# Writing out the loop over pairs of token tiles in the last stage of a two-layer kernel

## What is computed

```python
x = x + L0_attn(layernorm(x), ...)   # state mixing with N = 16
x = x + L0_ffn(layernorm(x), ...)    # 9 experts, top 2
x = x + L1_attn(layernorm(x), ...)   # 16 heads, causal
x = x + L1_ffn(layernorm(x), ...)    # 64 experts, top 8, and a shared one
```

```python
shared = silu(xf @ Ws_up) @ Ws_down
aff = xf @ centroids.T
_, idx = top_k(aff + expert_biases, 8)
w = sigmoid(take_along_axis(aff, idx, axis=1));  w = w / (sum(w) + 1e-08)
cw = zeros((T, E)).at[arange(T)[:, None], idx].add(w)
h = silu(einsum('td,edf->etf', xf, W_up))
routed = einsum('etd,te->td', einsum('etf,efd->etd', h, W_down), cw)
return shared + routed
```

## Time and profile before

| What | Value |
|---|---|
| median of 3 runs (lowest, highest) | 1024.24 us (1022.57, 1024.37) |
| the profiled execution | 1021.6 us |
| its span | 1019.9 us |
| mean granted TensorE clock | 0.956 |
| PE busy | 946.4 us, 93% of the span |
| DVE busy | 825.4 us, 81% |
| ACT busy | 700.0 us, 69% |
| POOL busy | 480.2 us, 47% |

### The profile page before, as it was taken

How to read it: one execution, slowest core, us unless ns; L and a number is a source line. 1 busy time by engine, 2 the same in 40 slices (tenths; PEclk the granted TensorE clock), 3 DMA queues, 4 the chain that set the end, 5 groups by cost and what they waited for, 6 DMA issues and landing times.

```text
span 1019.9 us, 20123 instructions
## 1 busy us (share of the span) xinstructions
PE 946.4 (93%) x6082; PEld 754.9 (74%) x6115; DVE 825.4 (81%) x1938; ACT 700.0 (69%) x1394; POOL 480.2 (47%) x550
## 2 busy tenths in 40 slices
PE   3686999999789999999999979999999999999997
PEld 2564998999657677767776657787877777778786
DVE  6888776777778888888887668989898889898865
ACT  3763554555467777877787657777777778777875
POOL 3278782107456565656553404444444444444443
PEclk8765999999779999999999999999999999999999
DMA  8994332222201110110010008493939292939291
GB/s 258 403 386 167 109 95 67 69 66 69 60 24 28 30 29 23 29 33 24 22 32 12 1 16 197 97 210 82 213 76 220 72 222 66 213 76 219 70 228 42
DMA packets 69156, 111.00 MB, mean 109 GB/s; under 512 B 16783, under 2 KB 54706, under 8 KB 64962
## 3 DMA queue, kind: packets, MB, share of 16 engines
q1 hardware_dynamic: 64080, 100.72, 37.8%
q0 software_dynamic: 4384, 8.99, 2.8%
q10 hardware_dynamic: 594, 0.09, 0.0%
HBM read 70.90 MB, written 38.86 MB: 108 GB/s over the span
## 4 chain that ended last, share of the span: by engine, by line
PE 74%; DVE 16%; ACT 4%; issue 3%; DMA 1%; SPq 1%; DVEq 0%; POOLq 0%; ACTq 0%
PE ps L2494 6%; PE ps L2476 5%; PE ps L2477 5%; PE ps L2478 5%; PE ps L2495 5%; PE ps L2496 5%; PE ps L2199 3%; DVE nm L1919 3%; PE ps L2307 3%; PE ps L2329 3%; PE ps L2301 3%; PE ps L2346 3%; PE ps L2177 2%; PE ps L2179 2%; PE ps L2178 2%
## 5 line engine op out<-in xcount | busy, mean ns | idle before, releaser
L927 POOL TENSOR_TENSOR hl<-h,hh 128x512 fp32r<-128x512 f32 x128 | 166.8, 1303 | 247.8 <-ACT hh L1238 247.8
L1238 ACT ACTIVATE hh<-h 128x512 fp32r<-128x512 f32 (+1 forms) x264 | 165.4, 627 | 43.8 <-DVE h L2004 41.2
L2004 DVE TENSOR_TENSOR h<-ps,cwB 128x512 f32<-128x512 f32 x192 | 130.8, 681 | 31.0 <-ACT ps L1227 28.1
L1919 DVE TENSOR_REDUCE nm<-ps 128x4 f32<-128x512 f32 (+1 forms) x128 | 116.3, 951 | 38.0 <-PE ps L2329 35.9
L1227 ACT ACTIVATE ps<-ps 128x512 f32<-128x512 f32 x192 | 111.6, 581 | 25.6 <-PE ps L2478 24.8
L2476 PE MATMUL ps<-xh,wh 128*128 128x512 f32 x256 | 103.0, 403 | 0.0
L2494 PE MATMUL ps<-hh,wh 128*128 128x512 f32 x256 | 102.3, 400 | 0.6 <-POOL hl L927 0.6
L2011 DVE TENSOR_TENSOR hl<-h,hh 128x512 fp32r<-128x512 f32 (+1 forms) x136 | 95.9, 705 | 8.4 <-ACT hh L1238 8.1
L2495 PE MATMUL ps<-hl,wh 128*128 128x512 f32 x256 | 100.0, 390 | 0.0
L2477 PE MATMUL ps<-xl,wh 128*128 128x512 f32 x256 | 100.0, 390 | 0.0
L2478 PE MATMUL ps<-xh,wl 128*128 128x512 f32 x256 | 99.9, 390 | 0.0
(11 more groups left out here) (367 smaller groups left out, 2671.4 us busy)
## 6 DMA issues: line engine op xcount, KB each, us to landing
cwB<-cwd SPq DMA_DIRECT2D x32, 1536.0 KB, 13.8
ys<-zfill SPq DMA_DIRECT2D x13, 1536.0 KB, 22.6
cwd<-cwS SPq DMA_DIRECT2D x64, 96.0 KB
xb<-xs SPq DMA_DIRECT2D x72, 64.0 KB
ys<-yb SPq DMA_DIRECT2D x72, 64.0 KB
x_res<-in_L_attn_x_dram SPq DMA_DIRECT2D x4, 512.0 KB, 6.6
wst<-in_L_ffn_W_up_dram SPq DMA_DIRECT2D x32, 64.0 KB, 2.1
wst<-in_L_ffn_W_down_dram SPq DMA_DIRECT2D x32, 64.0 KB, 1.9
```

The costliest lines, as they stand in the source:

```text
L927: pool.tensor_tensor(hl4[:, slot(u), :], h4[:, slot(u), :], hh4[:, slot(u), :].bitcast(F32), op=ALU.subtract).then_inc(u_hlp, 1)
L1238: act.activation(hh4[r, slot(u), :], h4[r, slot(u), :], ACT.Copy).then_inc(u_hh, 1)
L1919: ins = dve.tensor_reduce(nm[:, u, 4 * g:4 * g + 4], o, axis=AX.X, op=ALU.max, negate=True)
L2004: dve.tensor_tensor(h4[:, slot(u), :], first, second, op=ALU.mult).then_inc(u_h, 1)
```

## The change

On the four engines, the loop of two rounds over a pair of tiles becomes an ordinary loop of the host program. The tiles 2 to 5 stand in the program one after another, with constant numbers.

```diff
@@ -419,7 +419,7 @@
             last = T // TT - 1
             tile(0, 0, None, True, True)
             tile(1, 1, (0, 0, 0), True, True)
-            with eng.Fori(1, (last - 1) // 2) as it:
+            for it in range(1, (last - 1) // 2):
                 tile(it * 2, 0, (it * 2 - 1, 1, it - 1), True, True)
                 tile(it * 2 + 1, 1, (it * 2, 0, it), True, True)
             tile(last - 1, 0, (last - 2, 1, last // 2 - 1), True, False)
```

## The result

| | before | after |
|---|---|---|
| median of 9 runs each | 1023.85 us (1021.67 to 1024.47) | 1020.62 us (1018.69 to 1021.72) |
| ratio | 1 | 0.9971, 95% interval 0.9962 to 0.9981 |
| profiled execution | 1021.6 us | 1020.8 us |
| its span | 1019.9 us | 1019.0 us |
| tiles 2 to 5 in it | 203.74 us | 201.12 us |

The forecast was 1021.5 us and 0.26% less; measured were 1020.62 us and 0.29% less. The ratio is estimated from the runs of both kernels and isn't the quotient of the two medians (0.9968). Its interval stands for 1.9 to 3.9 us.

The account below looks back on a forecast made before the run. PE, busy 97.9% or more, was taken as the bound, held up only by late VectorE. Branch 1.50 plus register sums 1.20 gave 2.70 us: 1024.24 - 2.7 = 1021.5 us, range 1018.5 to 1023.9 us.

Parts of the forecast that it names:

- The bound and the yardstick: PE bounds tiles 2 to 5; written-out tile 1, 50.26 us, is their length without the loop, whose cost is the excess.
- The branch: Start of tile 4: VectorE waits for instructions after the branch back, 1.95 us late; removing it gains 1.50 us.
- Rival B: Start of tile 4: something other than the branch made it long; gain only 1.20 us, time 1023.0 us; chance 0.05.
- The register sums: VectorE's sequencer adding up wait values, showing behind the statistics in tiles 2 to 5; constants gain 1.20 us.
- Rival A: VectorE's waits: constants may be no cheaper, only the branch pays; gain 1.50 us, time 1022.7 us; chance 0.12.
- The other engines: Register instructions on PE, ScalarE and GpSimd in tiles 2 to 5: removing them gains 0 us.
- Rival C: Tiles 2 to 5 become as short as tile 6, 50.12 us; gain 3.3 us, time 1021.0 us; chance 0.08.
- The longer program: Two tiles more of straight code on four engines: 2 more instruction packets than now, priced at 0 us.
- rival D: Straight code starves VectorE of instructions, up to 1.50 us each time; with four, time 1027.5 us; chance 0.06.
- The chances: Whole kernel: faster by over 0.2% 0.63, within 0.2% 0.31, slower by over 0.2% 0.06.

Follow-up runs that it names:

- v: Against the kernel before, only VectorE's program written out, the other three engines keeping the loop; tiles 2 to 5 took 201.17 us.
- l: Against the kernel before, TensorE, ScalarE and GpSimd written out, only VectorE keeping the loop; tiles 2 to 5 took 203.81 us.
- the hint: Kernel before with the loop's branch target named ahead, on four engines or VectorE only; tiles 2 to 5 202.10 and 202.19 us, tile 6 55.47 and 54.45 us.
- the probes: Changed kernel plus two-round loops of semaphore increments ending VectorE's and ScalarE's programs, with varied body lengths, then set places; tiles 2 to 5 201.41 and 201.24 us.
- m: Kernel before, loop kept, with VectorE's statistics after unit 28 instead of 3 and GpSimd's use after 29 instead of 5; tiles 2 to 5 took 201.50 us.
- r: Against the kernel before, tiles 2 to 5 written out on four engines, pair number still in a register; tiles 2 to 5 took 202.21 us.
- the second comparison: The change itself run again beside the kernel before on another chip; 1020.12 us, ratio 0.9978 (0.9967 to 0.9990).

## Why the prediction was right, and where it was off

- **The bound and the yardstick.** Right. The changed tiles came out at 50.25 to 50.31 us where the written-out tile 1 of before had 50.26. Nearly the whole forecast was this one comparison within one trace. Some luck was in the size: tile 1 with its statistics after unit 3 took 50.26 to 50.38 us in the ten executions of the table, and 50.26 is the shortest. With 50.38 the same sum would have given 2.2 us and not 2.7. By the four sums of the change the gain is 2.33 to 2.62 us. The medians differ by 3.23 us, more than the windows explain; the rest lies within the interval.
- **The branch, 1.50 us.** Right in size (1.53) and in place (VectorE, by `v` and `l`); that it is a wait for instructions is shown by the hint and the probes. The Trainium skill, page "Advanced Engine Details and Errata", section "Control Flow Timing", gives about 108 ns for a compare-and-branch. The probes come near that only where the target is still held, with 0.2 to 0.35 us from the branch to the next instruction; beyond that it is 2.4 to 3.7 us, and the measurement decides. Rival B is out. The step from 1.95 us of lateness to 1.50 us of loss, "part of that is slack", was too simple: 0.7 us of it was the statistics coming on top.
- **The register sums, 1.20 us.** Right in size: 1.09 us by themselves, 0.80 against the longest sum of the change. The mechanism is shown for tile 3, whose 0.5 us come behind the statistics and go with them (50.17 in `m`). Tile 5's part comes at that place in the kernel before and at another in `r`, so there the agreement of the number is partly luck. Rival A, constant waits that cost as much, is out.
- **The other engines, 0.** Right, by the two mirror kernels `v` and `l`.
- **Rival C, more than the yardstick.** Not by this change, whose tiles stayed at 50.25; its size, tile 6's 50.12 in every tile, is what moving the statistics reached.
- **The longer program, 0, and rival D.** Right in the price, wrong in the count. "2 more than now" were forecast for tiles 2 to 5; there were 15 packets of instructions before and 15 after. The prediction counted only the second round, with 5 packets; the first, from 708 to 810 us, had 10 on the two queues together. The kernel before from 710 to 912 us, then the changed one from 710 to 911:

```profile
q14 instruction: 11, 0.09, 0.2%
q8 instruction: 4, 0.07, 0.2%
```

```profile
q8 instruction: 7, 0.11, 0.3%
q14 instruction: 8, 0.07, 0.1%
```

  On q8 the loop saved three packets, and on q14 it cost three. A body that isn't held is fetched again in every round, and carries the register sums besides; that this is why is argued from the counts. D's mechanism exists, as the hinted loops show, with 3 to 4 us without instructions on VectorE in straight code. No kernel without a hint had it.
- **The chances.** Faster by over 0.2% had 0.63. Nine runs gave 0.29%, the second comparison 0.22% with an interval from 0.10 to 0.33%; 2.62 us by the windows are 0.26%, inside both. "Only just outside" what can be told was the right warning.

## What to carry to other kernels

When a trace has the same work both in a loop and written out, compare the two between fixed marks before costing anything: the difference is the loop's price, with all contention in it. A branch back is cheap as long as the body is still held (three groups of 128 instructions on VectorE and ScalarE here) and costs 2.4 to 3.7 us once it isn't, so look for idle time right behind the branch on the engine that the others wait for, and write out that engine alone. Extra work of a sequencer showed mainly where its engine was already behind. Moving a burst of small work to a sparse place can take away more of the same hold-up: here another 0.56 us over four tiles. And look at the yardstick in more than one execution, since 0.1 us in it is 0.5 us in a forecast over four tiles.

## What was not expected

- The gaps fit groups of 128 instructions, of which three are usable, on both engines; the branch back of a body of 347 instructions costs 0.3 us or 2.4 to 3.7 us by its place alone.
- The hint for the branch back pays at the branch and is paid for later: 3.99 and 3.00 us without instructions on VectorE, 35 us into the first tile behind the loop. PE's waiting then also brought its granted clock down, to 0.97 in the mean of the tile.
- It stays open why ScalarE's 347 were spared in the kernel before, as its place there isn't known, and whether a hint armed only in rounds that do branch back would be free.
